# An attention and expert kernel: context rows in two transfers, the first norm on ScalarE, six VectorE steps rewritten, the front reordered, the last rows by tile

## The reference

```python
x   : (16, 112, 256)      ctx : (16, 375, 256)
# layer 1: cross attention
n = layernorm(x); q = n @ Wq + bq; k = ctx @ Wk + bk; v = ctx @ Wv + bv
x = x + softmax(q @ k.T / 16) @ v                  # for each of the 16 batches
# layer 2: eight experts, all of them computed for every token
n = layernorm(x)
g = einsum('bsh,ehf->ebsf', n, w_gate); u = einsum('bsh,ehf->ebsf', n, w_up)
o = einsum('ebsf,efh->ebsh', silu(g) * u, w_down)  # 8 experts, 1024 hidden units
cw = softmax(n @ w_router) * softmax(n @ w_gating / 0.1); cw /= cw.sum(-1) + 1e-9
x = x + einsum('ebsh,bse->bsh', o, cw)
```

## Time and profile before

| | us |
|---|---|
| median of 3 runs (1015.11 to 1018.01) | 1017.58 |
| the profiled execution | 1015.27 |
| its span, first to last instruction | 1013.2 |
| busy in the span: PE / PEld | 984.0 / 938.2 |
| busy in the span: DVE / ACT / POOL | 762.5 / 474.7 / 689.8 |

### The profile page before, as it was taken

The page is one execution under the profiler, slowest core; times in us unless marked ns, Lnnn a source line. Parts: engine busy times, 40 slices in busy tenths (PEclk is TensorE's granted clock), DMA queues, the critical chain, the costliest instruction groups (busy, mean ns, idle before and its releaser), DMA issues.

```text
span 1013.2 us, 16479 instructions
## 1 busy us (share of the span) xinstructions
PE 984.0 (97%) x6178; PEld 938.2 (93%) x6178; DVE 762.5 (75%) x1333; ACT 474.7 (47%) x837; POOL 689.8 (68%) x522
## 2 busy tenths in 40 slices
PE   6788899999999999999999999999999999999998
PEld 5788889999999999999999999999999999999997
DVE  3888843787777778777777788777778877777785
ACT  3466555445453545454445445453545444445441
POOL 3789887586666757676766667666757676767642
PEclk8799999999999999999999999999999999999999
DMA  6322023001010101010010101010101010010002
GB/s 174 97 88 94 20 70 105 22 22 43 21 32 12 43 22 42 21 42 22 22 42 22 42 22 42 22 36 9 41 22 43 22 42 22 25 39 21 1 1 73
DMA packets 37503, 40.63 MB, mean 40 GB/s; under 512 B 2800, under 2 KB 35424, under 8 KB 37424
## 3 DMA queue, kind: packets, MB, share of 16 engines
q1 hardware_dynamic: 37424, 39.58, 12.5%
HBM read 35.90 MB, written 3.67 MB: 39 GB/s over the span
## 4 chain that ended last, share of the span: by engine, by line
PE 88%; POOL 4%; DVE 3%; DMA 2%; issue 1%; ACT 1%; SPq 1%; DVEq 0%; POOLq 0%; ACTq 0%
PE ps L262 87%; DMA xf<-in_L_xattn_Wv 2%; POOL early L392 1%; POOL arena L455 1%; DVE arena L266 1%; POOL early L380 1%; POOL arena L398 0%; DVE var L968 0%; SPq L274 0%; DVE xf L1075 0%; PE ps L1536 0%; DVE xf L1081 0%; POOL rstd L386 0%; PE ps L1455 0%; DVE bn L963 0%
## 5 line engine op out<-in xcount | busy, mean ns | idle before, releaser
L262 PE MATMUL ps<-arena 128*128 128x256 f32 (+4 forms) x3120 | 420.0, 288 | 11.8 <-DVE arena L1008 5.9
L262 PEld LDWEIGHTS ps<-arena 128*128 128x128 f32 (+2 forms) x3120 | 410.9, 193 | 18.8 <-DVE arena L1008 6.1
L455 POOL TENSOR_TENSOR arena<-shared,arena 128x448 fp32r<-128x448 f32 x196 | 251.4, 1298 | 196.1 <-ACT arena L770 185.4
L262 PE MATMUL ps<-xc_hi,w_hi 128*128 128x448 f32 x904 | 331.8, 367 | 0.2 <-DVE shared L1094 0.2
L262 PE MATMUL ps<-xc_hi,w_lo 128*128 128x448 f32 x904 | 330.3, 365 | 0.0
L262 PE MATMUL ps<-xc_lo,w_hi 128*128 128x448 f32 x904 | 329.8, 365 | 0.0
L763 ACT ACTIVATE shared<-shared 128x448 f32<-128x448 f32 x180 | 101.4, 579 | 192.0 <-DVE shared L1111 125.0
L262 PEld LDWEIGHTS ps<-xc_hi,w_lo 128*128 128x128 f32 x904 | 169.8, 188 | 13.9
L262 PEld LDWEIGHTS ps<-xc_hi,w_hi 128*128 128x128 f32 x904 | 170.5, 189 | 10.7 <-issue 0.3
L262 PEld LDWEIGHTS ps<-xc_lo,w_hi 128*128 128x128 f32 x904 | 170.6, 189 | 10.3
L1105 DVE TENSOR_TENSOR shared<-ps,shared 128x448 f32<-128x448 f32 x60 | 37.5, 625 | 111.0 <-PE ps L262 111.0
(11 more groups left out here) (132 smaller groups left out, 1126.8 us busy)
## 6 DMA issues: line engine op xcount, KB each, us to landing
early<-in_L_ffn_w_down SPq DMA_DIRECT2D x16, 512.0 KB, 4.0
shared<-in_ctx SPq DMA_DIRECT2D x16, 375.0 KB
w_raw<-in_L_ffn_w_gate SPq DMA_DIRECT2D x17, 256.0 KB, 2.9
w_raw<-in_L_ffn_w_up SPq DMA_DIRECT2D x17, 256.0 KB, 3.3
early<-in_L_ffn_w_gate SPq DMA_DIRECT2D x15, 256.0 KB, 2.9
early<-in_L_ffn_w_up SPq DMA_DIRECT2D x15, 256.0 KB, 3.3
x_dram<-xsacc SPq DMA_DIRECT2D x8, 224.0 KB, 2.5
xsacc<-x_dram SPq DMA_DIRECT2D x1, 1792.0 KB, 7.6
```

Source lines behind the costliest of these rows:

```text
L262: ins = nc.tensor.matmul(dst, w, m, start=first and i == 0, stop=last and i == len(passes) - 1, skip_group_check=onto)
L455: nc.gpsimd.tensor_tensor(h[:, 1, j, at:at + TC], tile, h[:, 0, j, at:at + TC].bitcast(fp32), ALU.subtract).then_inc(hid_lo_done, 1)
```

## The change

- **Transfers.** Each half of the context is loaded by two transfers, 112 partitions and 13, on one semaphore. SP's order in the front changes; the halves of the third pair stand ahead of the last x rows and of the first weight set, and the stores of x1 behind the last context half.
- **First norm.** `norm1` goes from GpSimd to ScalarE as `activation(Identity, bias, scale)`. For that VectorE makes the negated mean (16 instructions of one column) and GpSimd multiplies it by the root (5 instructions). `norm1` keeps its two waits, now in ScalarE's program.
- **VectorE steps.** Adding 1e-5 to the variances becomes a sum over three columns, of which the third was filled with 1e-5 (13 `tensor_scalar` become `tensor_reduce`). `qbias` is made by two one-column instructions. For the first token group the sums are made pair by pair with one operand in PSUM (`sums_of_pair`, six of 128x224), one of them into a free piece of `w_raw0`, and the last sum is made by GpSimd (`sum_s4`).
- **Order.** All five lists of the front are new. Three idle matmuls at the start (`keep_busy`) become seven, single or in pairs, six of them behind the first weights' transposes. The second `route` and four `down` calls stand earlier in the plain quads.
- **The end.** The last 42 matmuls go by tile of the hidden units; rows 4 to 6 are finished first, then 0 to 3; three stores instead of four.

```diff
             def load_ctx_half(p, b):
-                sp.dma_start(ctx_raw[:, p % 2, b], ctx_v[p][:, b]).then_inc(ctx_in[p % 2][b], DMA)
+                for rows in CTX_ROWS:
+                    sp.dma_start(ctx_raw[rows, p % 2, b], ctx_v[p][rows, b]).then_inc(ctx_in[p % 2][b], DMA)
+        CTX_ROWS = (slice(0, KP - KP % 16), slice(KP - KP % 16, KP))
...
             def root1(i, rows):
                 pool.wait_ge(stats1_done, i + 1)
                 nc.gpsimd.tensor_tensor(rstd1[:, rows], var1[:, rows], power_c[:, rows], ALU.pow).then_inc(root1_done, 1)
-            def norm1(p):
-                pool.wait_ge(root1_done, (1, 2, 3, 3, 4, 4, 5, 5)[p])
-                ...
-                    ins = nc.gpsimd.tensor_scalar(xn[:, b, :], xs[:, 2 * p + b, :], mv1[:, 2 * p + b, 0:1], rstd1[:, i],
-                                                  ALU.subtract, ALU.mult)
+                pool.wait_ge(root1_done, i + 1)
+                nc.gpsimd.tensor_tensor(bias1[:, rows], shift1[:, rows], rstd1[:, rows], ALU.mult).then_inc(bias1_done, 1)
+            def sum_s4():
+                pool.wait_ge(sum13[0], 2)
+                pool.wait_ge(part_lo[0, "s13"], 1)
+                nc.gpsimd.tensor_tensor(xf[:, 5:6, :], xf[:, 2:3, :], s2_first, ALU.subtract).then_inc(sum24[0], 1)
...
+            def norm1(p):                                     # ScalarE
+                sc.wait_ge(bias1_done, (1, 2, 3, 3, 4, 4, 5, 5)[p])
+                if p > 0:
+                    sc.wait_ge(xt_ready, p)
+                    sc.wait_ge(q_bk_done, p)
+                for b in range(2):
+                    i = slice(2 * p + b, 2 * p + b + 1)
+                    ins = nc.scalar.activation(xn[:, b, :], xs[:, 2 * p + b, :], ACT.Identity, bias=bias1[:, i], scale=rstd1[:, i])
+                ins.then_inc(xn_done, 1)
...
             def stats1(i):
-                nc.vector.tensor_scalar(var1[:, first:end], mv1[:, first:end, 1], EPS, None, ALU.add).then_inc(stats1_done, 1)
+                nc.vector.tensor_reduce(var1[:, first:end], mv1[:, first:end, 1:3], AX.X, ALU.add)
+                for b in range(first, end):
+                    ins = nc.vector.tensor_scalar(shift1[:, b:b + 1], mv1[:, b, 0:1], -1.0, None, ALU.mult)
+                ins.then_inc(stats1_done, 1)
             def stats2(p):
-                nc.vector.tensor_scalar(var2[:, p % 2, :], mv2[:, p % 2, :, 1], EPS, None, ALU.add).then_inc(stats2_done, 1)
+                nc.vector.tensor_reduce(var2[:, p % 2, :], mv2[:, p % 2, :, 1:3], AX.X, ALU.add).then_inc(stats2_done, 1)
+            def sums_of_pair(p):                              # p = 2, 3
+                ve.wait_ge(xf_done, p + 1)
+                cols = slice(p % 2 * TP, (p % 2 + 1) * TP)
+                nc.vector.tensor_tensor(xf[:, 5, cols], xf[:, 0, cols], ps_x2[:, 0, :], ALU.subtract).then_inc(s3_made, 1)
+                nc.vector.tensor_tensor(xf[:, 4, cols], xf[:, 3, cols], ps_x2[:, 0, :], ALU.add)
+                ve.wait_ge(s3_made, p - 1)
+                nc.vector.tensor_tensor(s2_first[:, 0, cols], ps_x2[:, 1, :], xf[:, 5, cols], ALU.subtract).then_inc(sum13[0], 1)
...
             def transpose_norm2(p):
+                if p in (3, 4):
+                    pe.wait_ge(sum13[0], p - 2)
...
             pe.wait_ge(lg_cleared, 1)
-            keep_busy(3)
-            pe.wait_ge(consts_set, 1)
+            transpose_weights(0)
             transpose_weights(1)
-            transpose_weights(0)
+            keep_busy(1)
+            keep_busy(1)
             merged_weights()
...
             pe.wait_ge(acc_done, RT * g)
             pe.wait_ge(act_done, last + HID11)
             pe.wait_ge(gate_sum, 5 * (QUADS - PLAIN))
             for i in range(RT):
                 last_rows(i, row_passes(g, i, 0), first=i % 2 == 0)
-            pe.wait_ge(hid_lo_done, 4 * QUADS)
-            for i in range(RT):
-                accumulate(ps_end[i], row_passes(g, i, 1), first=False, last=i % 2 == 1 or i == RT - 1).then_inc(row_ready, 1)
+            pe.wait_ge(hid_lo_done, last + HID11)
+            for i in range(3):
+                last_rows(i, of_tile(i, 0))
+            ...                                               # rows 4 to 6, then row 3, tile 0
+            pe.wait_ge(hid_lo_done, last + HID12)
+            for i in range(4):
+                last_rows(i, of_tile(i, 1), last=i % 2 == 1).then_inc(row_ready, 1)
```

More of the change, by code:

```diff
@@ new lines, in load_biases, with load_wv, load_bv @@
+            def load_biases():
+                with nc.allow_non_contiguous_dma("a few short rows"):
+                    for i, src in enumerate((bq, bk)):
+                        sp.dma_start(b_raw[:, i, :], src.rearrange("(k p) -> p k", p=P)).then_inc(biases_in, DMA)
+            def load_wv():
+                sp.dma_start(wv_raw, wv.rearrange("(k p) n -> p k n", p=P)).then_inc(wv_in, DMA)
+            def load_bv():
+                sp.dma_start(bv_all, bv[None, :].broadcast_to((TQ, D))).then_inc(bv_in, DMA)
@@ L306, in _, with load_router @@
+            def load_router():
+                with nc.allow_non_contiguous_dma("a few short rows"):
+                    for i, src in enumerate((w_router, w_gating)):
+                        sp.dma_start(wr_raw[:, :, i * E:(i + 1) * E], src.rearrange("(k p) n -> p k n", p=P)).then_inc(router_in, DMA)
+            load_weights(0)
+            load_weights(1)
+            load_x(0)
             load_ctx_half(0, 0)
-            with nc.allow_non_contiguous_dma("a few short rows"):
-                for i, src in enumerate((bq, bk)):
-                    sp.dma_start(b_raw[:, i, :], src.rearrange("(k p) -> p k", p=P)).then_inc(biases_in, DMA)
+            load_biases()
@@ L318, in _ @@
-            load_set(0)
[L319 to L323, removed]
+            load_x(1)
+            load_ctx_half(1, 0)
+            load_ctx_half(1, 1)
+            load_wv()
+            load_x(2)
+            load_bv()
@@ L832, in _ @@
[L832 removed]
             exponentials(4, 0)
+            normalise(3)
+            ct_high(5, 1)
             exponentials(4, 1)
[L835 removed]
+            q_high(5)
+            pt_high(4, 0)
             cn_high(5, 0)
+            pt_high(4, 1)
+            norm1(6)
+            ct_high(6, 0)
+            keep_norm2(1)
             cn_high(5, 1)
[L838 to L840 removed]
+            xt_high(6)
             at_high(3)
[L842 removed]
@@ L843, in _ @@
-            keep_norm2(1)
-            ct_high(6, 0)
+            high_part(0, "first")
             exponentials(5, 0)
+            ct_high(6, 1)
             normalise(4)
+            q_high(6)
             exponentials(5, 1)
-            xt_high(6)
-            at_high(4)
-            cn_high(6, 0)
+            norm1(7)
             pt_high(5, 0)
             pt_high(5, 1)
+            cn_high(6, 0)
             keep_norm2(2)
-            ct_high(6, 1)
-            q_high(6)
+            xt_high(7)
@@ L871, in _ @@
             pt_high(6, 1)
+            keep_norm2(3)
+            ct_high(7, 1)
+            high_part(0, "second")
+            q_high(7)
             high_part(0, "s13")
+            at_high(5)
+            normalise(6)
+            high_part(0, "s2")
             exponentials(7, 0)
             exponentials(7, 1)
-            normalise(6)
             pt_high(7, 0)
+            keep_norm2(4)
+            at_high(6)
+            plain_silu(0, 0)
             pt_high(7, 1)
-            at_high(6)
```

572 lines of the change are left out of this document (292 added, 280 removed).

## The result

| | before | changed |
|---|---|---|
| median, us (4 runs each) | 1016.65 (1015.11 to 1018.01) | 990.09 (988.13 to 992.14) |
| profiled execution / its span | 1015.27 / 1013.2 | 992.14 / 990.4 |
| start of the first scores | 25.78 | 17.33 |
| start of the loop | 182.57 | 159.4 |
| start of the last 84 matmuls | 999.69 | 976.39 |

The changed kernel is faster: ratio 0.974 (95% interval 0.971 to 0.977), 26.6 us. The prediction said 17 us, 1000.6, with a range down to 991. The result lies beyond that range, on the side of rival 3 (992.6). The profiled execution is the slowest of the four runs.

The account below looks back on a forecast made before the run. TensorE bounds the loop; only head and attention, with waits and low clock, can give. Head 6.3 plus attention 12.7 less costs 0.6, 1.0 and 0.4 is 17.0 us: 1017.58 falls to 1000.6 us, range 991 to 1010.

Parts of the forecast that it names:

- rival 3: Nearly all TensorE waits go: head 8, attention 18, costs 1, so 25 us off, 992.6 us; chance 13%.
- What bounds the kernel: TensorE is fully busy in the loop and nearly so in the plain quads; only head and attention can give.
- signs of being right: First scores at 19-20 us, halves under 2 us, variance steps 0.1-0.2 us, attention idle 6-7 us, plain quads without long gaps.
- signs of being wrong: ScalarE idle for `q_bk` while TensorE waits; a gap before the second `route`; clock under 0.9 after 40 us.
- Head, the step on the transfers: In the head, a context half takes about 1.5 us instead of 2.9; four come about 5 us earlier in sum.
- Attention, the step that failed: From 25.78 to 128 us, 8.1 us of waits go and 6.5 stay; with clock 12.7 us, bounds 4 and 19.
- Rival 1: Attention is bound by the chain within a pair; removed stops return as others, 4 to 5 us won, 1008.8; chance 20%.
- The clock: Between 25.78 and 128 us, fewer stops win back 4.5 of the 8.0 us lost to low clock.
- Rival 4: Slower: `norm1` waits in ScalarE's list hold up casts, 3 us per pair for seven pairs, 1021.6; chance 6%.
- Rival 2: The head does not move, through slow 13-row transfers or the norm's longer way; 10.7 us off, 1006.9; chance 12%.
- Costs: Time added: idle matmuls 0.6 us, plain quads with the earlier second `route` 1.0 us, the end 0.4 us.
- The variance steps: On VectorE in the attention, eight steps fall from 7.5 us to 0.15 each; three of four columns, 3.5 to 0.45.

Follow-up runs that it names:

- all four parts back: The changed kernel with one transfer per context half, variance steps as tensor_scalar, half sums from SBUF and first norm on GpSimd again: 1014.07 us, ratio 0.999.
- the last kernel: The changed kernel with only the second route spread between wide matmuls, the old end, and rows 4 to 6 ahead of the row-add wait: 983.35 us.

## Why the prediction was wrong, step by step

**What bounds the kernel** was read rightly: the loop gave 0.1 us, the head and attention everything.

**The account.** On the profiled executions it foresaw 17.0 and got 23.1 us. Head with its idle matmuls: 5.7 foreseen, 8.45 measured. Attention and plain quads: 11.7 foreseen, 14.7 measured. Loop: nothing foreseen, 0.1 measured. End: -0.4 and -0.5. Outside the span 0.3. The other 4.4 us of the miss are no mechanism: the median before lay 2.3 us above its profiled execution and was carried over, while the changed kernel's lies 2.05 us below its own, which had the two falls of the clock.

The signs that the prediction named came out mixed. All the signs of being right were met or passed. But two of its signs of being wrong appeared as well, a wait ahead of the second `route` (0.56 us) and a clock under 0.9 after 40 us (0.68 from 122 to 138 us), in a kernel that was faster than forecast.

**Head, the step on the transfers.** The size of a half was about right: 1.5 us taken, under 2 measured, against 2.9. Its reason was not: a half at the 173 GB/s that it names takes 2.2 us. Wv's cast behind the queries was right. Two terms were mis-sized. "I give 3.0 of the possible 4 us: the queries start at 15" was 14.01. And the idle matmuls were priced at 0.6 us of cost, for four calls more than before where the kernel has three more; without all six the scores start 3.5 us later. The prediction saw the queries at 2.87 us for twelve and never asked what they would take at full clock, which is 1.3 us less. It also charged the transfers with the head alone. The runs show 9 to 10 us for them in either order, 3.9 to 6.8 of it in the head and the rest behind it: in the new order where ScalarE waited for later halves and weights, in the old order in the clock.

The page "DMA: Bandwidth & Descriptors" of the Trainium skill, section on why a DMA increments its semaphore by 16, says that the engine count is the largest up to 16 that divides the slowest dimension. The trace agrees: a share of 0.32 with one transfer of 125 rows, 0.80 over a microsecond and 0.96 in its middle with 112 and 13.

**Attention, the step that failed.** "The other 6.6 are short ones between steps of a pair, and in them one late step replaces another; I leave 6.5." 2.5 were left. In all, 12.3 us of waits went where 8.2 were foreseen, and 1.2 us of low clock where 4.5 were; the plain quads cost 0.2 and not 1.0. That makes 13.3 of the 14.7 us, and the rest is not traced. The prediction had the loads of the other engines nearly right. Over the whole front, to the loop, GpSimd went from 136.4 to 118.3 us of work (18 less, 14 foreseen), VectorE from 117.2 to 100.0 (17 less, 10 foreseen), ScalarE from 96.4 to 104.0 (8 more, 7.5 foreseen). It drew the wrong limit from them, that 75 of 79.5 has "little slack": GpSimd is 90% busy between 30 and 100 us, and TensorE doesn't wait for it once. Rival 1, that the removed waits come back within a pair, is refuted, and rival 3 named what came about; its "against" was the mistaken sentence. In the new order the loads decide: the first norm back on GpSimd brings 7.5 us of waits back, and all four parts back leave 14.0 us of idle time. What the lighter engines would give in the old order isn't shown: only the transfers (15.1 us still idle) and the variance steps were tried there, each alone.

**The clock.** 3.5 us were left for it. In the profiled execution some 6.8 us are lost, all in or behind the router's matmuls, 5.1 of them where the 0.56 us wait stands ahead; in the profile of the last kernel, with the second route spread, none. That the clock was low after the long stops was right for before, and left out that it can fall with a short stop or with none.

**Rival 4** (norm1's waits in ScalarE's list) is refuted: ScalarE stood idle 2.6 us ahead of all sixteen. One takes 608 ns, not the 471 of the nearest row, which reads PSUM. Moving it there gave the most.

**Rival 2** is refuted by the head itself: 8.45 us.

**Costs.** A wait of 0.56 us ahead of the second route, of the 1.0 foreseen for the plain quads, is within its bounds; the fall of the clock behind it cost 5.1 us in the profiled execution and was in no term. The end was right in sign and size; it is below what the medians can tell.

**The variance steps** were taken at the right size (0.15 us; 158 ns measured), and the 7.3 us that they take off VectorE are worth 3.3 us of the total. The one-column steps were charged at 0.27 us each and take 0.144. The page "SBUF — State Buffer" of the Trainium skill, section "Who interferes with whom", says that VectorE and GpSimd share an exclusive port pair and that a VectorE instruction with two SBUF inputs contends with a GpSimd one that reads SBUF. The sum of 4.62 us, which ended with GpSimd's step, and its twin of 0.38 behind it agree; the three of 0.37 to 0.39 us beside GpSimd's two-column step show that not every meeting costs something.

## What to carry to other kernels

When several engines are loaded to 85 or 90% of the bound engine's time, the small waits between them can be a matter of load. The new order without the lighter steps gave 1.3 us, within its error, and every one of these steps cost 3 to 13 us when it was put back. So don't judge an order by a kernel whose steps are still heavy. An edit that only fills TensorE's gaps has to be priced at both clock levels, by the durations of the matmuls behind it. And the time that a transfer saves must be followed past the first consumer, through everything queued behind it.

## What the hardware showed that was not expected

- TensorE's granted clock fell to 0.50 (1.2 GHz) while it was busy without a gap, in a row of 28 matmuls of 16 columns (88.46 to 91.9 us), and again behind 16 of them after a 0.56 us wait. A matmul of 448 columns then took 0.57 us instead of 0.36, for 10 us. It doesn't happen in each execution of the same order: of the five runs of one kernel four took 986.2 to 986.7 us at a mean clock of 0.999 or 1.000, and the fifth 992.81 us at 0.995. Twenty such matmuls in a row with no wait ahead kept 1.00 in three profiles of three.
- A `tensor_scalar` on two or four columns took 0.17 us at best and up to 3.4 in the kernel before, 0.75 to 1.8 on average in its groups of three and of eight. The two kinds on one column never did: 0.14 us in all sixteen cases of one, 0.26 to 0.27 in all sixteen of the other.
- Six idle matmul calls, three of them ahead of the first scores, are worth about 3 us, while the clock column of the first 20 us reads 1.00 with and without them.
